# A tensor of their own for the broadcast reciprocal norms, folded attention weights kept in DRAM, and another order of the feed-forward tasks

## The reference

```python
h = shift_token(x)
q, k, v = split(h @ wqkv)              # 8 heads of 64
q, k = l2norm(q) * qs, l2norm(k) * ksc
q, k = rotary_xpos(q, k)
o = local_attention(q, k, v)           # windows of 64, own and previous window
x = x + o @ wo
h = layernorm(shift_token(x)) * lg + lb
a, g = split(h @ w1 + b1)
x = x + (a * gelu(g)) @ w2 + b2
```

## Time and profile before

| | us |
|---|---|
| median of 3 runs | 2268.1 |
| lowest and highest of them | 2256.44, 2269.57 |
| the profiled execution | 2281.34 |
| its span, first to last instruction | 2279.2 |
| PE busy | 1837.4 |
| DVE busy | 1444.4 |
| ACT busy | 1117.9 |
| POOL busy | 901.3 |

### The profile page before, as it was taken

How to read it: one execution, slowest core, us unless ns; L and a number is a source line. 1 busy time by engine, 2 the same in 40 slices (tenths; PEclk the granted TensorE clock), 3 DMA queues, 4 the chain that set the end, 5 groups by cost and what they waited for, 6 DMA issues and landing times. The chain is left out here.

```text
span 2279.2 us, 50236 instructions
## 1 busy us (share of the span) xinstructions
PE 1837.4 (81%) x20010; PEld 1120.2 (49%) x20074; DVE 1444.4 (63%) x2281; ACT 1117.9 (49%) x2070; POOL 901.3 (40%) x624
## 2 busy tenths in 40 slices
PE   1577888888888787799999996677788888887886
PEld 1344454544555454466666663344454544544543
DVE  2466766566665644688888885566666665555563
ACT  1134444354444433488888884234434444444342
POOL 2444444454444440222222222444544444444440
PEclk9888999899999989799999997789989898999899
DMA  3122223222222321000000000123322222233221
GB/s 123 36 59 61 69 70 93 62 60 66 68 68 73 84 60 29 1 2 1 2 1 2 1 1 1 46 60 87 76 60 60 61 73 60 70 90 77 64 65 42
DMA packets 60664, 118.84 MB, mean 52 GB/s; under 512 B 7519, under 2 KB 17939, under 8 KB 58259
## 3 DMA queue, kind: packets, MB, share of 16 engines
q1 hardware_dynamic: 60435, 115.64, 20.0%
HBM read 82.51 MB, written 3.74 MB: 38 GB/s over the span
## 5 line engine op out<-in xcount | busy, mean ns | idle before, releaser
L942 POOL TENSOR_TENSOR QK<-QK,SQ 128x1024 f32<-128x1024 f32 x128 | 298.3, 2352 | 190.6 <-DMA SQ<-norms_d 190.6
L782 DVE SCALAR_TENSOR_TENSOR TP<-bank,cols,tab 128x1024 f32<-128x1024 f32 x256 | 320.4, 1275 | 47.2 <-PE bank L447 34.5
L805 DVE TRANSPOSE_TENSOR_REDUCE MX<-bank 128x16 f32<-128x512 f32 x256 | 160.4, 684 | 264.6 <-PE bank L484 264.6
L936 POOL TENSOR_TENSOR QK<-TP 128x512 f32<-128x512 f32 x128 | 164.3, 1283 | 407.8 <-DVE TP L782 260.4
L1195 ACT ACTIVATE PL<-bank,NM 128x384 f32<-128x384 f32 (+3 forms) x512 | 255.5, 540 | 15.6 <-DVE NM L1275 12.7
L1275 DVE TENSOR_REDUCE NM<-bank 128x1 f32<-128x384 f32 (+3 forms) x352 | 217.7, 635 | 35.4 <-PE bank L1109 31.7
L475 PE MATMUL bank<-bandb,identb 128*128 128x512 bf16 x192 | 74.5, 510 | 180.8 <-POOL QK L942 178.0
L1118 PE MATMUL bank<-cst,PL 128*128 128x128 f32 x1280 | 200.0, 275 | 3.3 <-DVE PTL L1284 1.1
L639 ACT ACTIVATE SQ<-bank 128x512 f32<-128x512 f32 x128 | 76.5, 598 | 239.7 <-PE bank L447 239.7
L1104 PE MATMUL bank<-KL,QZL 128*128 128x384 f32 (+3 forms) x512 | 189.3, 422 | 2.3 <-DVE QZL L1232 2.3
L484 PEld LDWEIGHTS bank<-QK 32*64 32x64 f32 x8192 | 155.8, 162 | 40.8 <-issue 40.8
(11 more groups left out here) (171 smaller groups left out, 3777.1 us busy)
## 6 DMA issues: line engine op xcount, KB each, us to landing
SQ<-norms_d SPq DMA_DIRECT2D x128, 256.0 KB, 4.9
OT<-sums_d SPq DMA_DIRECT2D x128, 256.0 KB, 3.9
V<-V SPq DMA_DIRECT2D x32, 512.0 KB, 7.7
V<-V SPq DMA_DIRECT2D x32, 384.0 KB, 8.8
RB<-vars_d SPq DMA_DIRECT2D x32, 256.0 KB, 3.2
X<-in_L_attn_x SPq DMA_DIRECT2D x8, 256.0 KB, 4.4
out<-X SPq DMA_DIRECT2D x8, 256.0 KB, 8.5
wqkv_raw<-in_L_ffn_wqkv SPq DMA_DIRECT2D x1, 1536.0 KB
```

The lines of the kernel that those rows point to most:

```text
L782: nc.vector.scalar_tensor_tensor(out=TP[:, o:o + 2, :], in0=BK[4 + z][:, :].unsqueeze(1).to_broadcast([P, 2, T]), scalar=q, in1=tab[:, e, ...
L805: last = nc.vector.tensor_reduce(MX[:, i, :], BK[i][:, :].rearrange("p (a b) -> p a b", b=32), AX_X, ALU.max, apply_transpose=True)
L936: nc.gpsimd.tensor_tensor(QK[:, m, 0, :], TP[:, 2, :], TP[:, 1, :], ALU.subtract)
L942: nc.gpsimd.tensor_tensor(QK[:, m, :, :], QK[:, m, :, :], SQ[:, m, 1, :].unsqueeze(1).to_broadcast([P, 2, T]), ALU.mult).then_inc(S["nr_ok ...
```

## The change

It has four parts. The broadcast reciprocal norms get a tensor RB, so `square_b` waits only for PE's reading of SQ. To make room for it, the folded attention weights (Wq_s, Wk_s, Wv_s, 1152 floats per partition) become one setup tensor `fold`, which SP writes to DRAM in the setup and reads back at the start of `mla_phase`; U of `ffn_phase` has one buffer instead of two, and `stats` has 4 slots. The loop bodies of PE, ACT, DVE, POOL and SP list the tasks in another order and, for some, with another PSUM bank.

```diff
+        folded_d = nc.dram_tensor("folded_d", (P, 2 * GROUPS * P + P), F32).ap()
...
+                    sp.wait_ge(copied, 8)
+                    sp.dma_start(folded_d, fold[:, :]).then_inc(kept, 16)
+                    sp.wait_ge(kept, 16)
...
-                U = sb("U", [P, 2, NT, P])
+                U = sb("U", [P, NT, P])
...
+                RB = sb("RB", [P, 4, T])
...
-                                sp.dma_start(SQ[32 * i:32 * i + 32, :, 1, :],
+                                sp.dma_start(RB[32 * i:32 * i + 32, :, :],
                                              src.unsqueeze(0).broadcast_to([32, 4, T])).then_inc(S["r_in"], 16)
...
                         for n in range(-3, NU + 4):
+                            run(variances, n - 3)
+                            run(sums, n - 2, 0)
+                            run(sums, n - 2, 1)
+                            run(norms, n - 1)
+                            run(result, n - 4)
                             run(values, n - 1)
-                            run(result, n - 4)
-                            run(variances, n - 2)
-                            run(sums, n - 1, 0)
-                            run(sums, n - 1, 1)
-                            run(norms, n)
...
                             if u >= 1:
-                                act.wait_ge(S["nr_ok"], 4 * (u - 1) + m + 1)
+                                act.wait_ge(S["ss_in"], u)
                             nc.scalar.activation(SQ[:, m, 1, :], BK[5][:, :], ACT.Square).then_inc(S["sb_ok"], 1)
...
                             nc.gpsimd.tensor_tensor(QK[:, m, :, :], QK[:, m, :, :],
-                                                    SQ[:, m, 1, :].unsqueeze(1).to_broadcast([P, 2, T]),
+                                                    RB[:, m, :].unsqueeze(1).to_broadcast([P, 2, T]),
                                                     ALU.mult).then_inc(S["nr_ok"], 1)
...
+                        sp.dma_start(fold[:, :], folded_d).then_inc(S["fold_in"], 16)
...
                         xt(0)
+                        pe.wait_ge(S["fold_in"], 16)
```

More of the change, by code:

```diff
@@ L579, in _ @@
                         for n in range(-3, NU + 4):
-                            run(hidden, n - 3, 1, 0, 5)
-                            run(hidden, n - 3, 1, 1, 7)
-                            run(back, n - 4, 4)
-                            run(tokens, n + 1, 4)
-                            run(join, n - 2, 6)
+                            run(project, n - 1, 1)
+                            run(add_max, n - 2, 0)
+                            run(hidden, n - 4, 0, 1, 7)
+                            run(hidden, n - 4, 0, 2, 6)
@@ new lines, in _ @@
+                            run(project, n - 1, 2)
+                            run(scores, n - 2, 1)
+                            run(sums, n - 2, 0, 6)
+                            run(project, n - 1, 3)
+                            run(turn_max, n - 2, 1, 6)
+                            run(outward, n - 4, 7)
+                            run(add_max, n - 2, 1)
+                            run(norms, n - 1, 6)
+                            run(attend, n - 2, 0, 5)
+                            run(sums, n - 2, 1, 4)
@@ new lines, in _ @@
+                            run(back, n - 4, 7)
+                            run(tokens, n, 7)
+                            run(hidden, n - 3, 1, 0, 6)
+                            run(attend, n - 2, 1, 5)
+                            run(attend, n - 2, 2, 4)
+                            run(attend, n - 2, 3, 5)
+                            run(values, n - 1, 0, 6)
+                            run(values, n - 1, 1, 7)
+                            run(values, n - 1, 2, 6)
+                            run(values, n - 1, 3, 7)
@@ L585, in _ @@
+                            run(hidden, n - 3, 1, 1, 6)
+                            run(hidden, n - 3, 0, 0, 4)
+                            run(join, n - 2, 7)
                             run(project, n, 0)
                             run(scores, n - 1, 0)
-                            run(center, n - 2, 7)
-                            run(project, n, 1)
-                            run(hidden, n - 3, 1, 2, 6)
-                            run(variance, n - 2, 7)
-                            run(turn_max, n - 1, 0, 6)
@@ L592, in _ @@
-                            run(hidden, n - 3, 0, 0, 7)
-                            run(add_max, n - 1, 0)
-                            run(hidden, n - 3, 0, 1, 6)
-                            run(project, n, 2)
-                            run(scores, n - 1, 1)
-                            run(sums, n - 1, 0, 7)
-                            run(project, n, 3)
-                            run(turn_max, n - 1, 1, 6)
-                            run(hidden, n - 3, 0, 2, 7)
-                            run(add_max, n - 1, 1)
@@ L602, in _ @@
-                            run(attend, n - 1, 0, 6)
-                            run(norms, n, 7)
-                            run(attend, n - 1, 1, 4)
-                            run(sums, n - 1, 1, 7)
-                            run(outward, n - 3, 5)
-                            run(attend, n - 1, 2, 4)
-                            run(attend, n - 1, 3, 6)
-                            run(values, n, 0, 5)
-                            run(values, n, 1, 7)
-                            run(values, n, 2, 5)
@@ L612, in _ @@
-                            run(values, n, 3, 7)
+                            run(center, n - 2, 6)
+                            run(hidden, n - 3, 1, 2, 7)
+                            run(variance, n - 2, 6)
+                            run(turn_max, n - 1, 0, 7)
                     @block.scalar
@@ L884, in _ @@
                         for n in range(-3, NU + 4):
-                            run(gated, n - 4, 1, 6)
+                            run(gated, n - 4, 2, 6)
                             run(rotate, n - 1, 2, 1)
@@ L960, in _ @@
                         for n in range(-3, NU + 4):
+                            run(norms, n - 3, 3)
+                            run(rotate, n - 2, 1)
+                            run(rotate, n - 2, 2)
                             run(hidden, n - 4)
+                            run(tokens, n - 1)
                             run(rotate, n - 2, 3)
                             run(low_hidden, n - 4)
-                            run(tokens, n)
                             run(low, n - 1)
@@ L969, in _ @@
                             run(rotate, n - 1, 0)
-                            run(norms, n - 2, 3)
-                            run(rotate, n - 1, 1)
-                            run(rotate, n - 1, 2)
                 stack.pop()
```

116 lines of the change are left out of this document (61 added, 55 removed).

## The result

The changed kernel takes **2337.8 us** (median of 3, 2337.41 to 2347.97) against 2268.1 before: ratio **1.0337**, 95% interval 1.027 to 1.0405, so 3.4% slower. Its profiled execution has a span of 2345.9 us against 2279.2, 66.7 us more. I read the same views as before, in the same order.

A forecast was written before the change was run, and what follows sets the result against it. The prediction took a closed chain, period A + L, as the bound. Per network -4.2 + 2 x 3 + 4 x 5.2 + 9 x 1.4 + 1 = 36 us, twice 73, forecast 2341 us; range 2260 to 2385.

The forecast's parts named there:

- L: Part of each iteration from the end of PE's sum of squares to the next `scores` 0: 22.1 us before the change.
- A: Part of each iteration from the start of `scores` 0 to the end of PE's sum of squares: 25.6 us before.
- the additions to DVE's row: Tasks moved into DVE's work after `scores` 0, such as `rotate` 1,1 (+1.2 us) and `gated` (+0.7), delaying `maxima` 1.
- edges: Network start and end: first `project` 0 earlier, -4.2 us; last units' chain +1 us, per network.
- the steps: Six forecast times in a layer 1 iteration, from CB's end at 9.6 us to the sum of squares' end at 27.3.
- Layer 1, +1.4 forecast: Average growth of A per layer 1 iteration, in us, from DVE's later row; bounds +0.7 and +2.5.
- Layer 0, +5.2 and +3 forecast: Growth per iteration in us: 5.2 in units 2 to 5 (1.4 + 1.1 + 2.7), 3 in units 0 and 1.
- 1.1, 2.7 and 3.8: Layer 0, units 2 to 5, in us: `statistics` on the chain 1.1, `tokens` delaying VN 2.7, and both together.
- RB at 0: Broadcasting the norms into RB instead of SQ costs or gains 0; bounds 1 us either way, 30 us in all.
- `fold` and the rest at 0: Writing and reading `fold`, single U and smaller `stats` add 0; at most 3 us for the write, 2 for the read.
- The faster one: Rival: broadcasts into a separate RB land sooner; if L fell by 4.5 us, 2206 us; chance 0.14.
- Nothing on balance: Rival: DVE's additions hide, `tokens` isn't held up and the start gains, giving 2282 us; chance 0.18.

The follow-up runs named there:

- writes_first: Kernel before, with SP's write of the norms issued right behind the write of `sums` 1, ahead of its wait and broadcasts: 2190.9 us, ratio 0.9642.
- project1_early: Changed kernel with PE's `project` 1 behind `center` and DVE's `rotate` 1,1 ahead of `add_eps` again: 2346.5 us, ratio 1.035.
- outward_behind: Changed kernel with `outward` behind `sums` 1 on PE and behind `norms` on DVE, PE's `back` and `tokens` moved too: 2353.3 us, ratio 1.0392.
- order_mended: Changed kernel with `project` 1 and `rotate` 1,1 early, `outward` behind `norms`, `tokens` behind `attended` 1, `statistics` behind `attended` 3: 2324.6 us, ratio 1.0256.

## Why the prediction came out right, step by step

**Right by its mechanism, and the number with some luck.** L was not shortened by RB, A grew, and the additions to DVE's row did it. But the order alone, which was to cost all of the 3.2%, costs 2.2 to 2.5% (50 to 57 us of the 73 forecast); the storage, forecast at 0, brings the rest (19 to 25 us) and fills the gap. By parts, forecast and measured: layer 1 25 and 8 us, units 2 to 5 42 and 38, units 0 and 1 12 and 20, edges -6 and +1. Errors of -17 and -4 and of +8 and +7 nearly cancel.

In the unit at 476.06 the steps stand as written (us after `scores` 0, forecast first): CB ends at 9.6 / 10.1; `maxima` 1 starts at 18.8 / 18.9; `rotate` 3,1 at 21.5 / 21.7, waiting for POOL; CB ends at 23.7 to 24.2 / 23.9; `add_max` starts at 24.3 / 24.3; the sum ends at 27.3 / 27.4. CB at 484.08 was held 0.53 us beyond the end of POOL's product (486.18 against 485.65), exactly as in the earlier trace rows. That unit has one of the faster `scores` 0 (clock 0.64). In most units of layer 1 `maxima` 1 starts 19.6 to 20.0 us after `scores` 0 and `add_max` 1 at 25.0 to 25.4: the clock over `scores` 0 is 0.50 to 0.57 there, and the steps follow 0.7 to 1.1 us late.

**Layer 1, +1.4 forecast, +0.45 measured.** The term furthest off is this one, mis-sized by a factor of three: it took no account of slow sums of squares. The comparison unit before had a fast clock; I had corrected only for a late `scores` 1. In 4 of the 18 units before, A is 29.9 because the clock is low during the sum of squares (3.5 us in place of 1.9). The mean A of the other 14 is 26.6, and against it the 28.1 of the changed kernel is +1.5, the step's own size. After the change no unit of layer 1 has that slow sum. It fits that `outward` now keeps PE busy just ahead of it, and the two runs that take `outward` away have 32 and 27 slow ones. So the step was right and the gain beside it was missing. L is 0.3 us shorter as well, which has no run of its own.

**Layer 0, +5.2 and +3 forecast, +4.7 and +5.0 measured.** In units 2 to 5 the split is near as well: A grew by 2.6 (26.7 to 29.3; forecast 1.4 + 1.1) and L by 2.1 (22.9 to 25.0; forecast 2.7). The sum of squares ends 29.3 us after `scores` 0 in the unit at 317.15, not 28.4, since `maxima` 1 starts at 19.9 behind a slow `scores` 0. What the moves are worth when undone is another matter. Putting back `statistics` gave 2.1 us in these units, `tokens` 4.2, both 5.3, so more than the forecast's 1.1, 2.7 and 3.8, and not a plain sum. With both back, units 2 to 5 have 49.0 against 49.6 before, and units 0 and 1 51.5 against 49.7. So layer 1's steps cost nothing visible in units 2 to 5: PE waits only 2.1 us before `scores` 0 in the units of layer 0 and mostly runs it faster. `tokens` standing still beside POOL (2.97 against 1.11 us) and VN late by 2.56 are as forecast. For units 0 and 1 I had left out slow sums of squares: each of these four iterations has one now (3.5 to 3.6 us), behind a wait of 3.58 us for CB, where before only one of the four had (3.38).

**Edges.** The fill gained 6.5, not 4.2. The last network's end takes 7.5 more, where I had +1: within the last unit alone `add_max` 1 comes 21.1 us after `scores` 0, before 17.8, and the clock over the tail behind it is 0.81 to 0.86, before 0.91 to 1.00. No run isolates the tail.

**RB at 0**: confirmed by two pairs of runs, to within their intervals of some 0.5%. **`fold` and the rest at 0**: not confirmed. The read of `fold` is indeed hidden in the trace, since PE waits 7.48 us for U at the start of the attention as it did before (7.49) and 0.88 us for the copy behind it. Yet kernels with only the storage changed are 0.8 to 1.1% slower. Which part, or whether it is the program's layout and not an operation, stays open.

**Two readings of the prediction were too wide.** The 178.0 us are 46% of what PE waits for in the two networks (some 390 us), not more than half. And not every DVE instruction on SBUF alone stands still beside POOL: in the changed kernel those of `statistics` (L292, L294) take 0.26 and 0.18 us with POOL at work and 0.28 and 0.18 without, while one of `tokens` goes from 0.34 to 1.29 and CB from 0.68 to 2.11 (medians).

**The rivals.** The faster one fell: nothing landed sooner. It had the right target, as `writes_first` shows: an earlier issue of the norms is worth 3.6%, 2.1 us a unit in L and 0.8 in A, but through the queue order of SP, not through the tensor. "Nothing on balance" fell mainly on layer 0; in layer 1 it nearly came true.

**What the prediction lacked** is a rule for PE: it treated a wait as time lost and nothing more. That made the remedies (`project1_early`, `outward_behind`, `order_mended`) look good and fail.

## What to carry to other kernels

Before moving a small task, ask what the other engine on the shared path does at that moment: four instructions of 1.1 us cost 3 us beside POOL, and held up a chain through another engine's queue. When PE has a latency to wait out, what fills the gap matters by itself; a task that looks like a delay inside the chain may be what keeps the clock up. And in a queue that carries a write, its wait and the reads of several chains, issue every write as soon as its data are there, before waiting for another chain.

## What the runs showed of the hardware

With a gap of 2.02 us before `scores` 0, on the other hand, the matmuls behind it ran at full speed, and behind gaps of 3.30 us both was seen (1.00 and 0.64). No row here tells which gaps count. In the kernel before, all 32 waits before `scores` 0 (3.1 to 7.3 us) were followed by a clock of 0.50 to 0.68 over it.
- 18 useless matmuls in each unit's gap made the kernel 2.0% faster (clock 0.951 against 0.915).
- The same four broadcasts took 7.1 us from issue to use in a unit where OT's were issued 4.7 us ahead of them, and 9.3 us in one where it was 1.7 us; the means over 32 units are 7.5 and 9.1.
- Beside POOL, CB took 2.11 us instead of 0.68 and one of `tokens` 1.29 instead of 0.34 (medians, changed kernel). `rotate`, which reads PSUM, took the same with POOL and without (1.28 and 1.27), and so did the batch-norm statistics from SBUF (0.26 and 0.28).
